# Three products of 256 columns in place of one of 512 and one of 256, in an attention and feed-forward kernel on one Trainium2 core

## The reference

```python
p1 = attn_map(q[:, :, :, 0], k[:, :, :, 0])       # causal softmax(q k / sqrt(128))
p2 = attn_map(q[:, :, :, 1], k[:, :, :, 1])
p = p1 - lam * p2
o = jnp.einsum('bhqk,bkhe->bqhe', p, v)            # the products with the values
rms = jax.lax.rsqrt(jnp.mean(o * o, axis=-1, keepdims=True) + EPS)
o = o * rms * subln_w
...
return o @ out_w.T + out_b
...
x_up = x @ W_up.T * (Wscale_ug[:INTER] * SCALE)
x_gate = x @ W_gate.T * (Wscale_ug[INTER:] * SCALE)
x = jax.nn.silu(x_gate) * x_up
x = fwht(x * SU_dp) / SCALE
x = x @ W_down.T * (Wscale_dp * SCALE)             # the second feed-forward product
...
x = x + _layernorm(_L0_attn_ref(_layernorm(x, axis=-1), ...), axis=-1)
x = x + _layernorm(_L0_ffn_ref(_layernorm(x, axis=-1), ...), axis=-1)
```

## Time and profile before

| | |
|---|---|
| median of 3 runs (lowest, highest) | 1406.95 us (1406.65, 1408.01) |
| the profiled execution | 1406.82 us |
| its span, first to last instruction | 1405.0 us |
| granted TensorE clock, mean | 0.997 |
| TensorE matmuls, busy and count | 1355.8 us, 8280 |
| TensorE weight loads | 1198.9 us, 8280 |
| VectorE | 1017.9 us, 2564 |
| ScalarE | 892.8 us, 2503 |
| GpSimd | 875.1 us, 1370 |

### The profile page before, as it was taken

How to read it: one execution, slowest core, us unless ns; L and a number is a source line. 1 busy time by engine, 2 the same in 40 slices (tenths; PEclk the granted TensorE clock), 3 DMA queues, 4 the chain that set the end, 5 groups by cost and what they waited for, 6 DMA issues and landing times.

```text
span 1405.0 us, 26355 instructions
## 1 busy us (share of the span) xinstructions
PE 1355.8 (96%) x8280; PEld 1198.9 (85%) x8280; DVE 1017.9 (72%) x2564; ACT 892.8 (64%) x2503; POOL 875.1 (62%) x1370
## 2 busy tenths in 40 slices
PE   5799999999999999999999999999999999999998
PEld 4679999988989999888889999888889888887887
DVE  5677778777677777767777788767678888855544
ACT  5467766766567667666666666665667777655442
POOL 2457666664757665555666756546767778758454
PEclk9999999999999999999999999999999999999999
DMA  3000000000000000000000000000100000000001
GB/s 131 2 31 1 1 1 1 1 16 1 1 31 1 1 1 1 1 16 2 31 1 1 1 1 1 20 1 1 46 1 1 22 26 1 17 30 1 27 15 35
DMA packets 9751, 18.49 MB, mean 13 GB/s; under 512 B 912, under 2 KB 7312, under 8 KB 9104
## 3 DMA queue, kind: packets, MB, share of 16 engines
q1 hardware_dynamic: 8272, 15.23, 3.2%
q10 hardware_dynamic: 1344, 1.57, 0.3%
HBM read 14.71 MB, written 2.10 MB: 12 GB/s over the span
## 4 chain that ended last, share of the span: by engine, by line
PE 75%; DVE 9%; POOL 7%; ACT 6%; issue 3%; DMA 0%; ACTq 0%; POOLq 0%; DVEq 0%
PE turn_bank L691 8%; PE score_bank L669 7%; PE score_bank L671 7%; PE score_bank L670 7%; PE score_bank L786 5%; PE sum_bank L691 4%; PE turn_bank L693 4%; PE turn_bank L678 3%; PE proj_bank L691 3%; PE turn_bank L737 3%; PE turn_bank L751 2%; ACT e L815 2%; PE sum_bank L693 2%; PE proj_bank L678 2%; POOL e L1257 2%
## 5 line engine op out<-in xcount | busy, mean ns | idle before, releaser
L815 ACT ACTIVATE e<-score_bank,negmx 128x512 f32<-128x512 f32 (+2 forms) x640 | 394.5, 626 | 82.2 <-DVE negmx L1029 81.5
L1257 POOL TENSOR_TENSOR e<-e,e 128x512 f32<-128x512 f32 (+3 forms) x256 | 295.7, 1155 | 21.4
L1025 DVE TENSOR_REDUCE mx<-score_bank 128x1 f32<-128x512 f32 (+1 forms) x384 | 244.8, 639 | 23.9 <-PE score_bank L671 22.9
L669 PE MATMUL score_bank<-k_hi,q_hi 128*128 128x512 f32 (+2 forms) x640 | 253.3, 396 | 7.8 <-ACT e L815 5.8
L1240 POOL TENSOR_TENSOR inv_s<-s,neg_one 128x1 f32<-128x1 f32 x128 | 71.1, 555 | 299.7 <-DVE s L1224 299.2
L671 PE MATMUL score_bank<-k_hi,q_lo 128*128 128x512 f32 (+2 forms) x640 | 231.7, 362 | 0.0
L670 PE MATMUL score_bank<-k_lo,q_hi 128*128 128x512 f32 (+2 forms) x640 | 231.1, 361 | 0.0
L691 PE MATMUL turn_bank<-v_hl,pT_hi 128*128 128x512 f32 x588 | 217.3, 403 | 5.6 <-DVE pT_lo L1035 5.5
L1254 POOL TENSOR_SCALAR e<-e,ratio 128x512 f32<-128x512 f32 (+3 forms) x256 | 178.1, 696 | 12.0
L1020 DVE CUSTOM_DVE_ANT_0 score_bank<-score_bank,mask 128x384 f32<-128x384 f32 (+3 forms) x256 | 143.4, 560 | 49.2 <-PE score_bank L671 47.8
L693 PE MATMUL turn_bank<-v_hl,pT_lo 128*128 128x256 f32 x588 | 165.0, 281 | 0.0
(11 more groups left out here) (347 smaller groups left out, 3551.3 us busy)
## 6 DMA issues: line engine op xcount, KB each, us to landing
w_raw<-in_w_qkv_dram SPq DMA_DIRECT2D x3, 1024.0 KB, 4.8
w_raw<-in_w_o_dram SPq DMA_DIRECT2D x4, 512.0 KB, 3.2
w_raw<-in_w_ug_dram SPq DMA_DIRECT2D x4, 512.0 KB, 3.9
bv<-in_hidden_dram SPq DMA_DIRECT2D x8, 256.0 KB, 3.0
out_dram<-e SPq DMA_DIRECT2D x16, 128.0 KB, 1.7
e<-in_w_d_dram SPq DMA_DIRECT2D x1, 1024.0 KB, 4.9
x_in<-in_hidden_dram SPq DMA_DIRECT2D x2, 256.0 KB, 3.8
x_in<-in_hidden_dram ACTq DMA_DIRECT2D x2, 256.0 KB, 4.2
```

Of the source, the lines that this page charges most:

```text
L669: pe.matmul(bank[:, 0:w], qh, kh, start=True, stop=False)
L815: act.activation(e, S[k % NS][:, 0:w], ACT.Exp, bias=negmx[:, d % 2, m, s:s + 1], accum_out=ssum[:, d % 4, s, m, c:c + 1]).then_inc(s_act, 1)
L1025: dve.tensor_reduce(mx[:, d % 2, m, s, c:c + 1], S[k % NS][:, 0:w], X, ALU.max)\
L1257: pool.tensor_tensor(a, a, b, ALU.add).then_inc(p_pool, 1)
```

## The change

Each block of PV and of DN is now three matmuls of 256 columns, hi·hi, hi·lo and lo·hi, into columns 0 to 255 of the bank. The halves need no addition: ScalarE copies the finished sum straight to o_sum and signals o_ready, and VectorE's PV step is gone. In DN, ScalarE's copy and VectorE's addition are both gone; statistics and `finish` read the PSUM bank itself, so the bank is free after d_scaled, which comes with the `finish` of that tile, in place of d_sum_ready. The semaphores o_half_ready, d_half_ready and d_sum_ready are gone (their declarations are left out below).

```diff
--- before.py
+++ after.py
@@ -81,7 +81,7 @@
 MIXES_A_STEP = 1
 
 SCALAR_LAGS = {'K': 1, 'V': 1, 'X': 1, 'QP': 0, 'OP': 0}
-VECTOR_LAGS = {'PV': 1, 'T': 1, 'OT': 1, 'Z': 1, 'F': 1, 'WO': 1, 'K': 1, 'V': 1, 'X': 1, 'FH': 1, 'U': 1}
+VECTOR_LAGS = {'T': 1, 'OT': 1, 'Z': 1, 'F': 1, 'WO': 1, 'K': 1, 'V': 1, 'X': 1, 'FH': 1, 'U': 1}
 
 
 FFN_CHUNKS = SEQ // BANK
@@ -431,7 +431,6 @@
                     return ap[:, tt // 2, tt % 2 * P:(tt % 2 + 1) * P]
                 return ap[:, tt * P:(tt + 1) * P]
 
-            d_half, d_sum = o_half, o_sum
             d_out = e2
             after = placer(nc, ssum_at)
             d_st = after("d_st", [P, 2, 6])
@@ -631,7 +629,7 @@
                     elif last and last[0] in ("K", "V"):
                         pe.wait_ge(kv_dve, kv_use[last] + 1)
                     elif last and last[0] == "DN":
-                        pe.wait_ge(d_sum_ready, last[1] + 1)
+                        pe.wait_ge(d_scaled, last[1] + 1)
                     elif last:
                         pe.wait_ge(o_ready, last[1] + 1)
                     return bank_for(*use)
@@ -688,10 +686,12 @@
                         pe.wait_ge(t_lo, t_use["T", what] + 1)
                         for b in range(w // P):
                             kt = first + b
-                            pe.matmul(bank[:, :], pT_hi[:, q % PT_SLOTS, b * P:(b + 1) * P], v_hl[:, kt, :],
-                                      start=(kt == 0), stop=False)
-                            mm = pe.matmul(bank[:, 0:HID], pT_lo[:, q % PT_SLOTS, b * P:(b + 1) * P],
-                                           v_hl[:, kt, 0:HID], start=False, stop=(kt == i))
+                            p_hi = pT_hi[:, q % PT_SLOTS, b * P:(b + 1) * P]
+                            p_lo = pT_lo[:, q % PT_SLOTS, b * P:(b + 1) * P]
+                            v_hi, v_low = v_hl[:, kt, 0:HID], v_hl[:, kt, HID:2 * HID]
+                            pe.matmul(bank[:, 0:HID], p_hi, v_hi, start=(kt == 0), stop=False)
+                            pe.matmul(bank[:, 0:HID], p_hi, v_low, start=False, stop=False)
+                            mm = pe.matmul(bank[:, 0:HID], p_lo, v_hi, start=False, stop=(kt == i))
                         mm.then_inc(pv_done, 1)
                     elif kind == "K":
                         g, m, c = what
@@ -795,9 +795,11 @@
                             pe.wait_ge(t_lo, t_use["F", 11] + 1)
                         bank = free_bank(kind, what)
                         for jt in range(JT):
-                            pe.matmul(bank[:, :], h_tile(c, jt, 0, tt), wd_hl[:, jt, :], start=(jt == 0), stop=False)
-                            mm = pe.matmul(bank[:, 0:HID], h_tile(c, jt, 1, tt), wd_hl[:, jt, 0:HID], start=False,
-                                           stop=(jt == JT - 1))
+                            h_hi, h_lo = h_tile(c, jt, 0, tt), h_tile(c, jt, 1, tt)
+                            w_hi, w_low = wd_hl[:, jt, 0:HID], wd_hl[:, jt, HID:2 * HID]
+                            pe.matmul(bank[:, 0:HID], h_hi, w_hi, start=(jt == 0), stop=False)
+                            pe.matmul(bank[:, 0:HID], h_hi, w_low, start=False, stop=False)
+                            mm = pe.matmul(bank[:, 0:HID], h_lo, w_hi, start=False, stop=(jt == JT - 1))
                         mm.then_inc(d_full, 1)
 
             @block.scalar
@@ -835,9 +837,10 @@
                         if last:
                             act.wait_ge(pv_done, CHUNKS * d + j + 1)
                             if o >= 2:
+                                act.wait_ge(t_full, t_use["OT", o - 2] + 1)
                                 act.wait_ge(msq_ready, o - 1)
-                            act.activation(o_half[:, o % 2, :], bank_for(kind, o)[:, HID:2 * HID], ACT.Copy)\
-                               .then_inc(o_half_ready, 1)
+                            act.activation(o_sum[:, o % 2, :], bank_for(kind, o)[:, 0:HID], ACT.Copy)\
+                               .then_inc(o_ready, 1)
                     elif kind == "OT":
                         o, u = what, t_use[kind, what]
                         act.wait_ge(t_full, u + 1)
@@ -983,14 +986,6 @@
                             act.wait_ge(d_full, QB * (c - 1))
                         act.activation(h_of(c, jt)[0], h_source(c, jt, h_f[:, what % 2, :]), ACT.Copy)\
                            .then_inc(h_hi_ready, 1)
-                    elif kind == "DN":
-                        act.wait_ge(d_full, what + 1)
-                        if what == 0:
-                            act.wait_ge(msq_ready, 2 * ALL_DUOS)
-                        if what >= 2:
-                            act.wait_ge(d_sum_ready, what - 1)
-                        act.activation(d_half[:, what % 2, :], bank_for(kind, what)[:, HID:2 * HID], ACT.Copy)\
-                           .then_inc(d_half_ready, 1)
 
             @block.vector
             def _(dve):
@@ -1002,7 +997,7 @@
                         dve.wait_ge(p_dve, dve_mixed[-1])
                     if n >= 4:
                         dve.wait_ge(stored[n % 4], 16 * (n // 4))
-                    dve.scalar_tensor_tensor(out=d_out[:, n % 4, 0:HID], in0=d_sum[:, x, :], scalar=d_rs[:, x:x + 1],
+                    dve.scalar_tensor_tensor(out=d_out[:, n % 4, 0:HID], in0=bank_for("DN", n)[:, 0:HID], scalar=d_rs[:, x:x + 1],
                                              in1=acc[:, tile, :], op0=ALU.mult, op1=ALU.add).then_inc(d_scaled, 1)
                     dve.wait_ge(d_scaled, n + 1)
                     dve.tensor_scalar(d_out[:, n % 4, 0:HID], d_out[:, n % 4, 0:HID], d_mr[:, x:x + 1], None,
@@ -1035,16 +1030,6 @@
                         dve.tensor_tensor(pT_lo[:, q % PT_SLOTS, 0:w], bank_for(kind, what)[:, 0:w],
                                           pT_hi[:, q % PT_SLOTS, 0:w].bitcast(F32), ALU.subtract)\
                            .then_inc(t_lo, 1)
-                    elif kind == "PV":
-                        d, j = what
-                        o, _, _, _, _, last = duo_chunks(d)[j]
-                        if last:
-                            dve.wait_ge(o_half_ready, o + 1)
-                            if o >= 2:
-                                dve.wait_ge(t_full, t_use["OT", o - 2] + 1)
-                                dve.wait_ge(msq_ready, o - 1)
-                            dve.tensor_tensor(o_sum[:, o % 2, :], bank_for(kind, o)[:, 0:HID],
-                                              o_half[:, o % 2, :], ALU.add).then_inc(o_ready, 1)
                     elif kind == "OT":
                         o, u = what, t_use[kind, what]
                         dve.wait_ge(t_hi, u + 1)
@@ -1203,13 +1188,10 @@
                            .then_inc(h_ready, 1)
                     elif kind == "DN":
                         x = what % 2
-                        dve.wait_ge(d_half_ready, what + 1)
+                        dve.wait_ge(d_full, what + 1)
                         if what >= 2:
                             dve.wait_ge(d_final, what - 1)
-                        dve.tensor_tensor(d_sum[:, x, :], bank_for(kind, what)[:, 0:HID], d_half[:, x, :],
-                                          ALU.add).then_inc(d_sum_ready, 1)
-                        dve.wait_ge(d_sum_ready, what + 1)
-                        dve.bn_stats(d_st[:, x, :], d_sum[:, x, :]).then_inc(d_stats, 1)
+                        dve.bn_stats(d_st[:, x, :], bank_for(kind, what)[:, 0:HID]).then_inc(d_stats, 1)
                         dve.wait_ge(d_stats, what + 1)
                         dve.bn_aggr(d_mv[:, x, :], d_st[:, x, :]).then_inc(d_aggr, 1)
                         if what >= 1:
```

More of the change, by code:

```diff
@@ L464, in build @@
              s_full, s_act, s_dve, t_full, t_hi, t_lo, r_full, r_hi, r_free, kv_full, kv_act, kv_dve, v_lo,
-             neg_ready, sums_ready, ratio_step, ratio_ready, e2_scaled, p_pool, p_dve, pv_done, o_half_ready, o_ready,
+             neg_ready, sums_ready, ratio_step, ratio_ready, e2_scaled, p_pool, p_dve, pv_done, o_ready,
              msq_ready, rms_step, rms_ready) = semaphores(
@@ L470, in build @@
                 "r_hi", "r_free", "kv_full", "kv_act", "kv_dve", "v_lo", "neg_ready", "sums_ready", "ratio_step",
-                "ratio_ready", "e2_scaled", "p_pool", "p_dve", "pv_done", "o_half_ready", "o_ready", "msq_ready",
+                "ratio_ready", "e2_scaled", "p_pool", "p_dve", "pv_done", "o_ready", "msq_ready",
                 "rms_step", "rms_ready")
@@ L474, in build @@
              y_rstd, z_rstd, z_ready, wsd_landed, wd_landed, wd_pool, wd_dve, g_full, u_full, g_act, h_ready,
-             h_hi_ready, h_lo_ready, d_full, d_half_ready, d_sum_ready, d_stats, d_aggr, d_pool, d_rstd, d_scaled,
+             h_hi_ready, h_lo_ready, d_full, d_stats, d_aggr, d_pool, d_rstd, d_scaled,
              d_final) = semaphores(
@@ L478, in build @@
                 "n_step", "n_scaled", "n_added", "n_pool", "y_rstd", "z_rstd", "z_ready", "wsd_landed", "wd_landed", "wd_pool", "wd_dve",
```

(3 more changed lines are left out.)

## The result

The changed kernel takes 1416.12 us (median of 5, 1414.62 to 1417.75) against 1408.01 us (median of 5): ratio 1.006, 95% interval 1.0049 to 1.007. In the later set it was 1416.96 against 1407.68, 1.0067 (1.0054 to 1.0079). So it is +8 to +9 us, slower as forecast; the forecast was +5.2. The time lies in the range of 1406 to 1418, but above the 1410 to 1414.5 to which the forecast gave 0.53.

What follows compares the result with a forecast made beforehand. TensorE, issuing nearly without a break, was taken to bound the kernel. Terms 6.0 + 1.1 − 0.9 + 0.45 − 0.45 − 1.0 = +5.2 us gave 1412 us, forecast 1410 to 1414.5, range 1406 to 1418.

Steps and rivals of the forecast that it cites:

- PV and DN triples: Attention PV and DN blocks on TensorE: three matmuls at 0.1185 us each, PV +6.0 us and DN +1.1.
- Tail: After the last DN tile: statistics start without ScalarE's copy and VectorE's addition, net −0.9 us.
- Wait for banks: Before the sixth DN tile: its bank is free only after VectorE scales the fourth, +0.45 us, once.
- Waits on o_sum: TensorE's wait near 1272 us: VectorE's addition goes since ScalarE's copy writes o_sum itself, −0.45 us.
- VectorE's relief: Fewer VectorE additions in attention: −1.0 us of pT_lo waits; as rival, 10 us idle given back, 1403.6, chance 0.09.
- columns alone: Rival for PV and DN: only columns cost, 2.4 us together, kernel about 1407.5 us, chance 0.24.
- The loads come to bind: Rival for PV and DN: the third weight load does not quite hide, 0.360 us a block, 1417.7 us, chance 0.14.

Runs made afterwards that it cites:

- e1: Kernel before with PV and DN as triples, hi·lo into the bank's second half, copy and addition kept: 1416.33 us, 1.0063.
- e7: Changed kernel with ScalarE copying the finished DN sum to SBUF, the bank free after that copy: 1415.01 us, 1.0054.
- e2: Changed kernel with the pairs of before (512 and 256 columns), hi·lo left out of the sum, no addition: 1409.2 us, 1.0009.
- e3: PV as in the changed kernel, DN as in the kernel before: 1414.49 us, 1.0053 against the kernel before.
- second profile: Another profiled execution of the unmodified changed kernel, at mean clock 0.997 like the profile before: span 1414.3 us.
- e4: Changed kernel with DN triples of 128 to 448 columns by tile, output not the reference's: 1423.06 us, one execution.
- e9: e1's program run once more for its profile: 124.31 us from last OP to last matmul, against 123.20 in e1.

## Why the prediction was right, and by how much it was short

- *PV and DN triples, +7.1.* The mechanism is right: with nothing else changed (e1, profiled span) it is +7.2. That the numbers meet so closely is partly luck. The triple was mis-sized, 0.1200 a matmul and not 0.1185, and so was the pair, 0.357 over the PV steps of group 1 and not the 0.350 read off two runs of eight blocks. The difference is 7.2 ns a block and not 5.5, about 7.8 us for PV and not 6.0. In DN the pair has 0.3533 in four of 16 tiles of the very profile that was read, so about 1.5 us and not 1.1. Against that, TensorE's longer steps ran into 1.4 us of its own waits. I had no term for that.
- *Tail, −0.9.* Right: −1.11, with about 0.2 more since GpSimd's small operations were shorter, too.
- *Wait for banks, +0.45.* Right for the sixth tile (the terms written down there give 0.38 to 0.41): 0.49 us are added between the fifth's last matmul and its first (1.40 after, 0.91 before). "Elsewhere three tiles lie between a bank's uses" was wrong. The two transposes take banks, so the seventh tile gets the fifth's, with one tile between, and is 1.28 us late. Together 1.8 (e7 takes them away by another release; e2 has them with pairs, e3, with DN as before, does not).
- *Waits on o_sum, −0.45.* Right at that wait, and worth nothing: 0.4 to 0.55 come back 17 us later in a wait on v_sum. *VectorE's relief, −1.0*: wrong, nothing (e2). It was read off waits that named VectorE, without following what VectorE itself waited for, which was ScalarE: its wkv_hi at the turns of a group, its pT_hi at 1242 us (e2).
- *Left out:* the stretch at the 1.2 GHz level behind the 2.2 us wait, 1.1 to 1.3 us where it occurs, and those before 90 us (+2.0 to the first marker, of which 272 blocks explain 1.6; +3.6 in the profiled execution of the result).

The sum for the second profile: 7.2 + 1.8 − 1.1 − 0.1 + 1.3 = 9.1, against 1414.3 − 1405.0 = 9.3. The direction came from the forecast mechanism. What was short is the bank waits (+1.35), a relief and a shorter wait that did not pay (+1.0 and about +0.4) and the clock (+1.3).

Of the rivals, columns alone is refuted, by the distances of 0.120 and by e4. The loads come to bind is right in its price for a block (0.360), in that there is a floor, and nearly in the time (1417.7; the measured 1416.1 is nearer to it than to the forecast's 1412). But e4 puts 256 columns above that floor, with the same 13 ns that 320 and 384 have. Which part of a matmul and its load makes up these 13 ns no run shows. VectorE's relief is refuted (e2).

## What to carry to other kernels

Where TensorE issues without a break, count instructions as well as columns: here each matmul of 256 to 384 columns in a triple cost about 13 ns beside its columns, and those of 128 to 224 columns cost 110 to 113 ns whatever their width. Read the price of a pattern over many steps: two runs of eight blocks gave 0.350 where the average was 0.357. Taking work from an engine that the bound engine rarely waits for gave nothing, 48 us of it (e2). When a PSUM bank is let go later, list the bank of every use in order; steps in between that take banks of their own can turn three tiles of slack into one. Compare idle time between the same places of the program: in a fixed window a wait can simply have moved out.

## What the runs showed of the hardware

- A matmul of 128, 192 or 224 columns costs nearly the same, 110 to 113 ns (e4); at 448 columns the part beside the columns is 19 ns, and in a run of 512 columns 21 (0.2345).
- A block of 512 and 256 columns takes 0.3467 or 0.3533 us, the same through a tile of eight blocks, and two executions of one program differ in how many tiles have which (4 and 15 of 16 at 0.3533).
- Two executions of the same program can differ by 1.1 to 1.3 us through one short stretch at 1.2 GHz behind a wait of 2.2 us (e1, e9), and by 1.5 through one before 50 us. Over 15 executions of the kernel before the span went from 1404.1 us at a mean clock of 0.998 to 1408.2 at 0.994.
